# A gated linear attention block with an FFN on one core: normalised rows turned by VectorE and DRAM instead of TensorE, and smaller tiles for the gate logits

## What is computed

```python
xn = layernorm(x)                       # mean, variance, eps 1e-5
q, k = elu(xn @ Wq) + 1, elu(xn @ Wk) + 1
v = xn @ Wv
a = sigmoid(xn @ Wa + ba + 2)           # a gate for each token and head
# for each head: S = a*S + k v^T, z = a*z + k, out = (q S) / (q z + 1e-6)
x = x + out @ Wo                        # 1024 -> 512
x = x + (layernorm(x) @ CB.T) * (SCB / 127) + bias
```

## Time and profile before

| | |
|---|---|
| three runs | 2017.58, 2018.64 (median), 2019.59 us |
| the profiled execution, its own time | 2018.3 us |
| its span in the profile | 2016.5 us |
| granted TensorE clock, mean | 0.997 of full speed |
| TensorE busy | 1989.3 us (99%) |
| VectorE busy | 1619.3 us (80%) |
| ScalarE busy | 684.3 us (34%) |
| GpSimd busy | 385.6 us (19%) |
| DMA packets | 461860, 220.62 MB, 41.5% of the 16 engines' time |

### The profile page before, as it was taken

One profiled execution on the slowest core, in us unless ns is written; L12 is line 12 of the kernel. 1 busy time (PEld: TensorE's weight loads), 2 busy tenths in 40 slices (PEclk: granted clock), 3 DMA queues, 4 the chain that ended last, 5 costly groups with the idle time before them and its releaser, 6 DMA issues.

```text
span 2016.5 us, 69510 instructions
## 1 busy us (share of the span) xinstructions
PE 1989.3 (99%) x27422; PEld 1718.6 (85%) x27422; DVE 1619.3 (80%) x2918; ACT 684.3 (34%) x1288; POOL 385.6 (19%) x368
## 2 busy tenths in 40 slices
PE   8999999999999999999999999999899999999998
PEld 7888888888888888888888888888677777777776
DVE  8888888888888888888888888888856666566565
ACT  5333433443343344334334434434311111111111
POOL 3211223322222332212233212222100000000000
PEclk9999999999999999999999999999999999999999
DMA  6343434444343444334344433435544433434442
GB/s 211 86 95 95 113 96 106 106 103 94 95 113 96 107 104 104 94 95 113 96 107 105 103 94 95 115 95 121 135 122 125 116 116 122 125 114 117 123 123 81
DMA packets 461860, 220.62 MB, mean 109 GB/s; under 512 B 296832, under 2 KB 412032, under 8 KB 461824
## 3 DMA queue, kind: packets, MB, share of 16 engines
q1 hardware_dynamic: 461824, 220.15, 41.5%
HBM read 168.59 MB, written 51.44 MB: 109 GB/s over the span
## 4 chain that ended last, share of the span: by engine, by line
PE 95%; SPq 2%; issue 1%; DVE 1%; DMA 1%; POOL 0%; ACT 0%; POOLq 0%; DVEq 0%
PE G L1267 51%; PE DS L1224 18%; PE NUM L1224 9%; PE NUM L1336 3%; PE SC L1212 3%; PE SC L1389 3%; PE DS L1368 3%; PE NUM L1350 3%; PE DS L1409 1%; SPq L393 1%; SPq L415 0%; DMA abc<-decay_rows 0%; SPq L460 0%; SPq L469 0%; DMA norm_rows<-moments 0%
## 5 line engine op out<-in xcount | busy, mean ns | idle before, releaser
L1267 PE MATMUL G<-w_hi,xT_hi 128*128 128x512 f32 x1024 | 406.9, 397 | 0.9 <-DVE w_lo L880 0.9
L1267 PE MATMUL G<-w_lo,xT_hi 128*128 128x512 f32 x1024 | 399.6, 390 | 0.0
L1267 PE MATMUL G<-w_hi,xT_lo 128*128 128x512 f32 x1024 | 399.1, 390 | 0.0
L728 ACT ACTIVATE relu_t<-G 128x512 f32<-128x512 f32 x256 | 153.1, 598 | 445.7 <-PE G L1267 443.5
L1267 PE MATMUL G<-xT_hi,w_hi 128*128 128x256 f32 x1024 | 290.0, 283 | 0.0
L1267 PE MATMUL G<-xT_lo,w_hi 128*128 128x256 f32 x1024 | 289.8, 283 | 0.0
L1267 PE MATMUL G<-xT_hi,w_lo 128*128 128x256 f32 x1024 | 289.8, 283 | 0.0
L1267 PEld LDWEIGHTS G<-w_hi,xT_hi 128*128 128x128 f32 x1024 | 192.4, 188 | 41.8 <-DVE xT_lo L873 1.0
L1267 PEld LDWEIGHTS G<-w_hi,xT_lo 128*128 128x128 f32 x1024 | 192.2, 188 | 41.4
L1267 PEld LDWEIGHTS G<-w_lo,xT_hi 128*128 128x128 f32 x1024 | 192.6, 188 | 35.8
L1224 PE MATMUL DS<-w_hi 128*128 128x512 f32 x512 | 207.4, 405 | 2.6 <-DVE w_lo L918 2.3
(11 more groups left out here) (136 smaller groups left out, 3800.2 us busy)
## 6 DMA issues: line engine op xcount, KB each, us to landing
abc<-decay_rows SPq DMA_DIRECT2D x256, 128.0 KB, 3.0
pbc<-product_rows SPq DMA_DIRECT2D x256, 128.0 KB, 3.1
attn_cols<-attn SPq DMA_DIRECT2D x512, 64.0 KB, 2.2
at_rows<-attn_cols SPq DMA_DIRECT2D x256, 128.0 KB, 2.7
xt<-in_x SPq DMA_DIRECT2D x64, 256.0 KB, 3.1
x_in<-in_x SPq DMA_DIRECT2D x64, 256.0 KB, 3.1
out_rows<-xt SPq DMA_DIRECT2D x64, 256.0 KB, 3.0
xT_in<-in_xT SPq DMA_DIRECT2D x31, 512.0 KB, 4.3
```

The lines of the kernel that those rows point to most:

```text
L728: act.activation(relu_t[buffer][:, :], bank[:, :], ACT.Relu)
L1267: made = nc.tensor.matmul(to, lhs, rhs, start=(n == 0), stop=(n == len(passes) - 1))
```

## The change

**Gate logits.** The weights are padded to GR = 32 columns instead of 64, and each product contracts over all 128 partitions, over 64 tokens. There are still 16 products for a pair; four of them (two stretches, two chunks) write to four groups of 32 partitions of one tile. So the sum of two halves is gone, and everything behind it works on 64 columns instead of 128: one scan instead of two, half the width for exponential and reciprocal. The gates are stored with one DMA of 128 partitions and the running products with four. The logits' products now come after `within(0)` on TensorE, not before it.

**Turning in phase 2.** For all chunks but the last, VectorE turns `x1n` in 32 x 32 blocks into `x1t`; ScalarE issues four DMAs that store its blocks to a new DRAM tensor `x1_cols`; SP loads the turned chunk with one DMA into `fT_in`; ScalarE and VectorE make its high and low part (now two buffers of each). TensorE has no transposes in these steps, and makes F of chunk i - 2 behind Y of chunk i. The last chunk is still turned by TensorE. The rows of the FFN weights are loaded in the order that the blocks give, with 16 DMAs instead of 4. The second chunk's rows are split one step earlier than before.

```diff
-    decay_rows = nc.dram_tensor("decay_rows", [NC, H * C], fp32).ap()
+    x1_cols = nc.dram_tensor("x1_cols", [NC, C * DM], fp32).ap()
+    decay_rows = nc.dram_tensor("decay_rows", [NC // 2, 4 * GR * L], fp32).ap()
...
# SP, FFN weights
-                    sp.dma_start(raw_wf[kt], CBT[128 * kt:128 * kt + 128, :]).then_inc(wf_loaded, 16)
+                    for x in range(4):
+                        at = 128 * x + SQ * kt
+                        sp.dma_start(raw_wf[kt][x:128:4, :], CBT[at:at + SQ, :]).then_inc(wf_loaded, 16)
...
# SP, step2
+                if exists(i + 2):
+                    sp.wait_ge(rows_loaded, r64[1])
+                    for h in range(2):
+                        sp.wait_ge(oT_lo_ready[h], one[0])
+                    load_attn(chunk_at(i + 2), b)
+                if exists(i + 1):
+                    sp.wait_ge(xin_loaded, x16[0])
+                    sp.wait_ge(x1_ready, one[-1])
+                    load_x(chunk_at(i + 1), 1 - b)
+                if turning:
+                    sp.wait_ge(x1t_stored, r64[-1])
...
+                    sp.dma_start(fT_in[1 - b].rearrange("p j c -> p (j c)"),
+                                 x1_cols[bass.ds(chunk_at(i - 1), 1), :].rearrange("o (p c) -> (o p) c", p=128))\
+                        .then_inc(fT_loaded, 16)
...
# ScalarE, step2
-                act.wait_ge(fT_ready, one[-1])
-                act.activation(by_stretch(fT_hi), both_of(TF), ACT.Copy).then_inc(fT_hi_ready, 1)
+                if exists(i - 2):
+                    act.wait_ge(fT_loaded, x16[-2])
+                    if exists(i - 4):
+                        wait(act, F_ready, one[-4])
+                    act.activation(fT_hi[b], fT_in[b], ACT.Copy).then_inc(fT_hi_ready, 1)
+                if exists(i - 1) and exists(i):
...
+                    act.wait_ge(x1t_ready, one[-1])
+                    for g in range(4):
+                        q = SQ * g
+                        act.dma_start(x1_cols[bass.ds(before, 1), :]
+                                     .rearrange("o (f b t) -> (o f) b t", f=SQ, t=C)[:, :, q:q + SQ],
+                                     x1t[1 - b][q:q + SQ, :].rearrange("f (b t) -> f b t", t=SQ)).then_inc(x1t_stored, 16)
                 if exists(i + 1):
                     rows_hi(r64[1], one[-1], 1 - b)
...
# VectorE, step2, in this order
+                    residual_normal(one[-1], x1[1 - b], x1n[1 - b])
+                    nc.vector.transpose(x1t[1 - b], x1n[1 - b]).then_inc(x1t_ready, 1)
...
+                    dve.wait_ge(fT_hi_ready, one[-2])
+                    nc.vector.tensor_tensor(fT_lo[b], fT_in[b], fT_hi[b].bitcast(fp32), ALU.subtract)\
...
+                    nc.vector.tensor_tensor(y[1 - b], F[1 - b], x1b[1 - b], ALU.add).then_inc(y_ready, 1)
...
                 if exists(i + 1):
                     rows_lo(one[1], 1 - b)
                 if exists(i):
                     residual(one[0], x16[0], b)
...
# TensorE, gate_logits
-                        for c in range(2):
-                            for a in range(2):
-                                ps = slice(64 * a, 64 * a + 64)
-                                made = nc.tensor.matmul(DS[64 * c:64 * c + 64, U * a + ZC:U * a + 512], wa[ps, kt, :],
-                                                        xT_in[ps, kt, tokens(c)], start=(kt == 0), stop=(kt == KT - 1))
+                        for a in range(2):
+                            for c in range(2):
+                                g, t = GR * (2 * a + c), C * c + L * a
+                                made = nc.tensor.matmul(DS[g:g + GR, ZC:ZC + L], wa[:, kt, :], xT_in[:, kt, t:t + L],
+                                                        start=(kt == 0), stop=(kt == KT - 1))
```

More of the change, by code:

```diff
@@ L199, in gated_linear_attention_block @@
                         for w in (w_hi, w_lo))
-        fT_hi, fT_lo = (w[:, 3, 2, :].rearrange("p (j c) -> p j c", c=C) for w in (w_hi, w_lo))
+        fT_hi, fT_lo = ([w[:, 3, 2 + b, :].rearrange("p (j c) -> p j c", c=C) for b in range(2)] for w in (w_hi, w_lo))
+        fT_in = [t.rearrange("p (j c) -> p j c", c=C) for t in pieces(kT, 2)]
+        x1t = pieces(D, 2)
         x1 = [t[:, :] for t in relu_t]
@@ L573, in step2 @@
             def step2(i, _, b):
[L574 to L579, removed]
+                one = counts(sp, i, 1, (-3, -1, 0))
+                x16 = counts(sp, i, 16, (-2, 0))
+                r64 = counts(sp, i, 64, (-1, 1))
+                y16 = counts(sp, i, 16, (-4,))
@@ L589, in step2 @@
-                if exists(i - 2):
-                    wait(sp, y_stored, y16[-3])
-                    wait(sp, y_ready, one[-2])
-                    sp.dma_start(out_rows[bass.ds(before, C), :], y[b]).then_inc(y_stored, 16)
-            steps(sp, step2, 1, NC + 2)
+                        sp.wait_ge(oT_lo_ready[h], one[0])
[4 more added lines that the diff above has]
+                    load_x(chunk_at(i + 1), 1 - b)
@@ L595, in _ @@
+                if exists(i - 3):
+                    wait(sp, y_stored, y16[-4])
+                    wait(sp, y_ready, counts(sp, i, 1, (-3,))[-3])
+                    sp.dma_start(out_rows[bass.ds(row(sp, i - 3), C), :], y[1 - b]).then_inc(y_stored, 16)
+            steps(sp, step2, 1, NC + 3)
             sp.wait_ge(y_stored, 16 * NC)
@@ L1178, in step2 @@
+                if isinstance(i, int) and i == NC:
+                    dve.wait_ge(y_ready, NC - 2)
+                    with_bias(1 - b)
                 if exists(i + 1):
@@ L1181, in step2 @@
                     residual(one[0], x16[0], b)
-                if exists(i):
-                    residual_rest(one[0], b)
-                    residual_normal(one[0], b)
-                dve.wait_ge(F_ready, one[-1])
-                if exists(i - 3):
-                    wait(dve, y_stored, y16[-3])
-                nc.vector.tensor_tensor(y[1 - b], F[1 - b], x1b[1 - b], ALU.add).then_inc(y_ready, 1)
-            steps(dve, step2, 1, NC + 1)
+                    if isinstance(i, int) and i == 1:
+                        dve.wait_ge(bias_loaded, 16)
+                    residual_deviation(one[0], 1 - b)
+                if isinstance(i, int) and i == 1:
+                    ffn_weights_lo()
+            steps(dve, step2, 1, NC + 3)
         @block.tensor
```

227 lines of the change are left out of this document (123 added, 104 removed).

## The result

The changed kernel takes **2055.53 us** (median of 4 runs, 2054.30 to 2058.91), against 2018.25 us for the kernel before on the same chip: a ratio of 1.0186 with a 95% interval of 1.0171 to 1.0202. The forecast was 2043 us.

A forecast was written before the change was run, and what follows sets the result against it. TensorE was taken to set the pace in both phases before the change, an added ScalarE store loop in phase 2 after it. 2018.3 - 12.4 (gates) + 34.8 (loop) + 2 (start and end) = 2042.7, so 2043 us; range 1968 to 2066.

The forecast's parts named there:

- The loop that is added: Phase 2: ScalarE's four stores, its split, VectorE's sum to normalised rows, transposition; 9.36 us a step against 8.79, +34.8 us.
- TensorE's step without transposes: Phase 2: without eight transposes (0.59 us) TensorE needs 8.20 us a step, worth 36 us if nothing else became longer.
- The gate logits: Phase 1: a group of gate products takes 0.48 us instead of 0.88, over 31 pairs: -12.4 us.
- The four tiles do run side by side: Phase 1 gates, opposed rival: four 128x32 tiles run one after the other, +27 us instead of -12.4, 2082 us; chance 0.03.
- Start and end of phase 2: Stops at phase 2's start and end, later weights and an F still to do: +2 us booked, between -4 and +8.
- 12 x 0.43 = 5 us later: Phase 2's start: 16 DMAs instead of 4 bring the FFN weights, at 0.43 us for each extra one, 5 us later.
- The paragraph that counted what SP is moved past: Phase 2 steps: SP's load and result store, 0.4 us each, follow an earlier-issued attention load; no time anyone waits for.
- The path of the turned rows: Phase 2: stores, landing, SP's load, ScalarE's high part, next stores; 8.1 us, 1.2 shorter than the 9.36 us loop, costing nothing.
- The sign given for it: Profile sign that the 8.1 us store-and-load loop decides: ScalarE waiting for the load of kT in each phase-2 step.
- The clock: Phase 2 rival: TensorE's clock falls at each stop, step 9.8 us, about 2070 us; chance 0.05, shared with longer landings.
- SP and ScalarE issuing together: Phase 2 rival: the two hinder each other when issuing DMAs, one issue of 0.44 us a step, +27 us, 2070; chance 0.03.
- The sum: Whole kernel: 2018.3 - 12.4 + 34.8 + 2 = 2042.7 us, forecast as 2043 us, 1.2% slower.

The follow-up runs named there:

- first experiment: Changed kernel with ScalarE's split of the next attention rows moved ahead of its wait for the turned chunk and the four stores: 2032.66 us.
- third experiment: Changed kernel with a fifth store per phase-2 step from ScalarE, to a spare DRAM tensor: 2095.94 us.
- eighth experiment: Changed kernel with split ahead, weights in four DMAs, stores halved between SP and ScalarE, stores before the load's wait, VectorE's attention low part first: 1969.18 us.
- experiment four: Changed kernel with FFN weight rows laid out by the host, so SP issues 4 DMAs for them, not 16: 2047.87 us.
- fifth: Changed kernel with two of each step's four stores issued by SP, two by ScalarE at its old place ahead of the split: 2001.48 us.
- sixth: Changed kernel with ScalarE's split ahead of its stores, FFN weights in 4 DMAs, and two stores each on SP and ScalarE: 1985.73 us.

## Why the prediction was near, and where it was off

- **The loop that is added** was the heart of it and holds: forecast 3.0 + 2.02 + 3.63 + 0.71 = 9.36 us, measured 2.98 (issues and gap) + 1.95 + 3.63 + 0.71 and 0.17 of hop, less 0.06 of overlap, 9.38. Over 61 steps +36.2 where +34.8 was booked. That ScalarE issues this shape as slowly as SP (2.96 and 3.14 us for four) was the assumption on which all hung: 2.88. Experiments one and three show the mechanism, by taking the issues out of the ring and by adding one.
- **TensorE's step without transposes**: 8.20 forecast, 8.16 measured, but only in the eighth experiment.
- **The gate logits**: 0.48 us for a group was too low, it is 0.59. The row it came from, line 1368 in the earlier trace rows, has tiles of 64x64; these are 128x32. The term is -7.9 in the profiled execution and -9.2 over all kernels, for -12.4. The four tiles do run side by side; that rival is out.
- **Start and end of phase 2** is the term that was mis-sized: +2 was booked, +5.6 + 4.1 = +9.7 came, outside its own range of -4 to +8. The step that failed is "12 x 0.43 = 5 us later": the price of one issue came from a load of whole rows of x, while these go to every fourth partition and take 0.70 us each, 11.2 for sixteen, 8.8 more than the four of experiment four, which took 0.61 each. The chain was also another: not GpSimd's scaling (done by 1445.35, not 1453.9) but the attention stores queued behind on SP. The paragraph that counted what SP is moved past looked only at the loop. Experiment four gives 7.7 us back. At the end, TensorE waits 1.29 us for the last rows and 2.78 for the turned chunk 62, which comes back by DRAM at the same time, and then has two F's to do. No experiment was made on the end alone; in the eighth the second of these stops is gone and the stretch from Y of chunk 63 takes 20.3 us for 23.6.
- **The path of the turned rows**: forecast as a second ring of 8.1 us, 1.2 under the first. By the first experiment it is 9.1, only 0.3 under. The link that was mis-sized is the last store's landing: 2.2 us were taken from the earlier trace rows, and from the start of that store's issue to SP's load it was 3.7. In the changed kernel this costs nothing, which with 0.3 us to spare was luck, but it is why undoing the first ring gave 23 us and not 73. The sign given for it, ScalarE waiting for the load of kT in each step, was a bad one: the changed kernel shows it (176.4 us in 49 waits) and the first ring decides all the same.
- **The clock** stayed at 1.00 through the stops of about 1 us in each step of the changed kernel; that rival is out. A longer stop did cost something: in the third experiment one of 2.39 us, before Y at 1488.54, was followed by seven matmuls at 0.5 of full speed. **SP and ScalarE issuing together**: in the eighth experiment pairs start 0.01 us apart and take 1.35 and 1.55 us, against 1.35 for a pair of ScalarE's alone in the changed kernel; on average an issue of ScalarE's takes 0.60 us beside SP's and 0.59 alone, so next to no hindrance shows. What SP's issues did cost, in the fifth and sixth, is that they queue up on SP itself. The rule of the Trainium skill that the prediction cited here ("Perfetto Trace Analysis", section "DMA Instruction — HWDGE (DVE, Sync)", one block shared by both) costs nothing one can see at this rate.
- The sum: terms off by +4.5, +1.4 and +7.7 us, which is the 13.6 us between 2042.7 and the profiled 2056.3. The forecast's own range, 2016 to 2064, does not follow from its bounds: 2.6 to 3.3 us of issues and -4 to +8 at the start give 2012 to 2067.

The Trainium skill, "DMA: Bandwidth & Descriptors", section "Issuing engines are not separate DMA queues", has the time of initiation as usually small beside the DMA. For one DMA that is so by a factor of four or five here (0.59 of 2.8 us). But issues add up on their engine while landings overlap: four issues, 2.88 us, are as long as one landing.

## What to carry to other kernels

A DMA issue is an instruction of its engine, and what stands behind it in program order waits: before giving stores to an idle engine, close the ring from its next instruction back to the stores and add it up. Then look for the next ring at once: one that runs from a store's landing through a load's wait back to the next store on an in-order engine, and, once issues have moved to another queue, one over that queue's own issues. Here each fix uncovered the next, steps of 9.39, 9.08, 8.35, and only the last reached TensorE's 8.16. To tell whether a landing or the queue holds a load, compare the load's start with both: with the landing of what it waits for and with the end of its queue's issue before it. What broke these rings was cheap: an order of statements, a second semaphore, half of the issues elsewhere.

## What was not expected of the hardware

- Two kinds of ring look different. Where issues and arithmetic set the step it is steady (9.36 to 9.45 us in the changed kernel). Where a wait for a landing, of a store or of a load, is in it, steps vary from 8.5 to 9.5 us (first experiment) or 7.2 to 9.6 (sixth); the runs vary too in the fifth, 1993.96 to 2003.17. In these traces steps that vary went with DRAM in the ring.
- 32 rows of weights into every fourth partition take SP 0.70 us to issue; 128 rows into 128 partitions 0.45 to 0.75, so four times the DMAs took 4.5 times as long.
- The median landing of the same store was 2.8 us in the changed kernel and 3.5 with the split ahead, at nearly the same DMA share (0.67 and 0.68).
